# One core, a graph network in one launch: the ranks of the second edge sort made in the edge pass, where they were made beside the attention and the mixer pass

## What is computed

```python
xn = _layernorm(x)
x = x + gnn0(xn, [src, dst], edge_weight) + mix0(xn)     # messages = xn[dst] * w, summed by src
x = x + ffn0(_layernorm(x))                              # 32 experts, one per token
xn = _layernorm(x)
x = x + gnn1(xn, src, dst, deg ** -0.5) + mix1(xn)       # xn[src] summed by dst
x = x + ffn1(x)                                          # 6 experts, two per token
```

## Time and profile before

| | |
|---|---|
| median of 3 runs | 6301.56 us (6300.48 to 6309.79) |
| profiled execution | 6297.91 us, span 6295.7 us |
| PE busy | 5271.7 us, 84% |
| DVE busy | 3384.1 us, 54% |
| POOL busy | 3878.9 us, 62% |
| ACT busy | 1311.4 us, 21% |

### The profile page before, as it was taken

One profiled execution on the slowest core, in us unless ns is written; L12 is line 12 of the kernel. 1 busy time (PEld: TensorE's weight loads), 2 busy tenths in 40 slices (PEclk: granted clock), 3 DMA queues, 4 the chain that ended last, 5 costly groups with the idle time before them and its releaser, 6 DMA issues.

```text
span 6295.7 us, 87281 instructions
## 1 busy us (share of the span) xinstructions
PE 5271.7 (84%) x24977; PEld 4430.6 (70%) x24977; DVE 3384.1 (54%) x9879; ACT 1311.4 (21%) x2962; POOL 3878.9 (62%) x4349
## 2 busy tenths in 40 slices
PE   0165766499999999989999899999999999987894
PEld 0154655267777777777888787778887788866782
DVE  9866666445555555455446544555455554547223
ACT  0011111011111111133224322331112311111340
POOL 5767777765655555688888883316763167636006
PEclk9976888699999999999999999999999999998995
DMA  1022122233333333611001101223332144453324
GB/s 43 24 79 81 55 63 58 83 104 98 100 99 98 101 98 98 69 46 42 17 16 39 39 17 27 82 65 100 104 100 80 62 114 114 109 95 96 97 89 133
DMA packets 319773, 477.58 MB, mean 76 GB/s; under 512 B 99008, under 2 KB 240054, under 8 KB 319470
## 3 DMA queue, kind: packets, MB, share of 16 engines
q0 software_dynamic: 153136, 262.81, 17.0%
q1 hardware_dynamic: 166334, 211.17, 10.9%
HBM read 371.27 MB, written 102.33 MB: 75 GB/s over the span
## 4 chain that ended last, share of the span: by engine, by line
PE 68%; DMA 10%; POOL 8%; DVE 8%; issue 4%; ACT 1%; DVEq 0%; SPq 0%; ACTq 0%; POOLq 0%
PE bank L2384 18%; PE bank L2395 14%; POOL scratch_sorted L1013 7%; DMA scratch_sorted<-sb_FREE 6%; PE bank L2430 6%; PE bank L2445 6%; PE bank L2612 5%; PE bank L2594 5%; PE bank L2881 3%; PE bank L2737 3%; PE bank L2375 2%; DMA sb_rows<-scratch_xn,sb_row_of 2%; PE bank L2923 1%; DVE sb_STATE L1498 1%; DMA sb_HT<-scratch_ys,sb_srec 1%
## 5 line engine op out<-in xcount | busy, mean ns | idle before, releaser
L1020 POOL DMA_INDIRECT sb_rows<-scratch_xn,sb_row_of x1760 | 1718.4, 976 | 1430.9 <-PE bank L2430 605.5
L1013 POOL DMA_INDIRECT scratch_sorted<-sb_FREE x1564 | 1608.2, 1028 | 486.8 <-issue 330.6
L2395 PE MATMUL bank<-sb_work_FT,sb_W 128*128 128x250 f32 x4400 | 1008.9, 381 | 20.4 <-ACT sb_work_FT L1100 16.0
L1100 ACT ACTIVATE sb_HT<-bank,sb_cols 128x250 f32<-128x250 f32 x1333 | 553.7, 467 | 1979.1 <-PE bank L2594 1060.9
L2395 PEld LDWEIGHTS bank<-sb_work_FT,sb_W 128*128 128x128 f32 x4400 | 846.5, 193 | 135.7 <-ACT sb_work_FT L1100 23.5
L2384 PE MATMUL bank<-sb_W,sb_HT 128*125 128x256 f32 x4000 | 893.4, 380 | 0.7 <-ACT sb_HT L1100 0.7
L2384 PEld LDWEIGHTS bank<-sb_W,sb_HT 128*125 128x125 f32 x4000 | 752.5, 188 | 115.0 <-ACT sb_HT L1100 1.1
L2445 PE MATMUL bank<-sb_rows,sb_work_TM 128*125 128x257 f32 x1760 | 471.4, 392 | 72.7 <-DMA sb_rows<-scratch_xn,sb_row_of 72.2
L1822 DVE TENSOR_TENSOR sb_STATE<-sb_STATE,bank 125x257 f32 x440 | 185.5, 422 | 623.0 <-PE bank L2445 594.1
L1767 DVE TENSOR_TENSOR sb_FREE<-sb_FREE,bank 125x257 f32 x440 | 185.8, 422 | 620.1 <-PE bank L2430 584.8
L2430 PE MATMUL bank<-sb_rows,sb_work_TM 128*125 128x257 f32 x1760 | 440.1, 389 | 34.4 <-DMA sb_rows<-scratch_xn,sb_row_of 25.2
(11 more groups left out here) (392 smaller groups left out, 7008.5 us busy)
## 6 DMA issues: line engine op xcount, KB each, us to landing
sb_rows<-scratch_xn,sb_row_of POOLq DMA_INDIRECT x1760, 2.8
scratch_sorted<-sb_FREE POOLq DMA_INDIRECT x1564, 2.4
scratch_qT<-sb_work_QF SPq DMA_DIRECT2D x100, 250.0 KB
sb_work_QF<-scratch_qT SPq DMA_DIRECT2D x100, 250.0 KB
sb_work_XC<-in_x SPq DMA_DIRECT2D x50, 250.0 KB
sb_work_ZT<-scratch_xn SPq DMA_DIRECT2D x50, 250.0 KB
sb_W<-in_L_mix_W SPq DMA_DIRECT2D x9, 1024.0 KB
sb_work_XC<-scratch_zs SPq DMA_DIRECT2D x28, 256.0 KB, 2.6
```

The source lines that it names most:

```text
L1013: nc.gpsimd.indirect_dma_start(out=sorted_d[e], out_offset=bass.IndirectOffsetOnAxis(ap=pos[e][0:n, c:c + 1], axis=0), in_=rec[e][0:n, 2 * ...
L1020: nc.gpsimd.indirect_dma_start(out=rows[:, t % RING, 0:D], out_offset=None, in_=table, in_offset=bass.IndirectOffsetOnAxis(ap=row_of[:, t: ...
L1100: return nc.scalar.activation(dst, source, func, **k)
L2395: ins = nc.tensor.matmul(dst[:, b, :], w[:, k0 + k, 128 * (b0 + b):128 * (b0 + b) + 128], source[:, k, :], start=(n == 0), stop=(n == 2 * ...
```

## The change

The ranks of the second sort are no longer made in A0 and B0. In A0 the 25 rounds keep only the is-equal, which now also writes its sum (the counts); the running count, the copy and the predicated copy go. From these counts the groups and bases come as before, and a copy of the bases is kept. `sort_start` and `sort_place_second` go from B0; behind B0 the blocks of the edges are copied to a place that the clearing of `STATE` does not reach.

In C0 each of the 25 chain steps gets six DVE operations of 782 columns, for two blocks: two is-equals, two running counts that start from the block's base, and two predicated copies. Each stands alone between two units. After `body_c0(23)`, the last body with a chain, six operations make the slots, and the second scatter on POOL waits for them.

```diff
-            def sort_rank(e, k):
-
-                before = SORT_BASE[e] + PREPARED
-                dve.wait_ge(sort_step, k * 4 + before)
-                nc.vector.scalar_tensor_tensor(is_b, half, iota_b[:, bass.ds(k, 1)], step_of, ALU.is_equal, ALU.mult)\
-                    .then_inc(sort_step, 1)
-                nc.vector.tensor_tensor_scan(scan, is_b, tmp, 0.0, ALU.add, ALU.add).then_inc(sort_step, 1)
-                nc.vector.tensor_copy(packed[:, bass.ds(k, 1)], scan[:, EC - 1:EC]).then_inc(sort_step, 1)
-                nc.vector.copy_predicated(rank, is_b.bitcast(I32), scan).then_inc(sort_step, 1)
...
+            def sort_second_count(k):
+
+                dve.wait_ge(sort_step, k + SECOND_READY)
+                nc.vector.scalar_tensor_tensor(is_b, half, iota_b[:, bass.ds(k, 1)], step_of, ALU.is_equal, ALU.mult,
+                                               accum_out=packed[:, bass.ds(k, 1)]).then_inc(sort_step, 1)
...
+            def sort_second_keep():
+
+                dve.wait_ge(sort_step, SECOND_KEPT - 2)
+                nc.vector.tensor_copy(blk_kept, blk).then_inc(sort_step, 1)
+                nc.vector.memset(at_kept, 0.0).then_inc(sort_step, 1)
+
+            def sort_second_place(c, n):
+
+                j, stage = n % 2, n // 2
+                b = 2 * c + j
+                before = SECOND_KEPT + 6 * c + n
+                dve.wait_ge(sort_step, before - (0 if n == 5 else 1 if c or n else 0))
+                if stage == 0:
+                    ins = nc.vector.tensor_scalar(is_kept[j], blk_kept, iota_b[:, b:b + 1], None, ALU.is_equal)
+                elif stage == 1:
+                    ins = nc.vector.tensor_tensor_scan(counts_kept[j], is_kept[j], is_kept[j], base_kept[:, b:b + 1],
+                                                       ALU.add, ALU.max)
+                else:
+                    ins = nc.vector.copy_predicated(at_kept, is_kept[j].bitcast(I32), counts_kept[j])
+                ins.then_inc(sort_step, 1)
+
+            def sort_second_slots():
+
+                dve.wait_ge(sort_step, SECOND_PLACED - 6)
+                step, at, slot = steps(SECOND_PLACED - 6), at_kept, is_kept[0]
+                step(nc.vector.tensor_scalar(at, at, -1.0, None, ALU.add))
+                step(nc.vector.tensor_scalar(slot, at, 63.5, 1.0 / 128, ALU.subtract, ALU.mult))
+                step(nc.vector.tensor_scalar(slot, slot, ROUND, ROUND, ALU.add, ALU.subtract))
+                step(nc.vector.scalar_tensor_tensor(at, slot, -128.0, at, ALU.mult, ALU.add))
+                step(nc.vector.scalar_tensor_tensor(at, at, float(NS), slot, ALU.mult, ALU.add))
+                step(nc.vector.tensor_copy(pos[1], at))
...
-            def sort_start(k):
-
-                before = SORT_BASE[1] + BASED
-                for j, buffer in enumerate((is_b, is_b2)):
-                    nc.vector.tensor_scalar(buffer, blk, iota_b[:, bass.ds(2 * k + j, 1)],
-                                            base[:, bass.ds(2 * k + j, 1)], ALU.is_equal, ALU.mult)\
-                for j, buffer in enumerate((is_b, is_b2)):
-                    nc.vector.tensor_tensor(start, start, buffer, ALU.add)\
...
             def body_a0(i, slots, after):
-                rank_beside(i, 0)
+                count_beside(i, 0)
...
-                rank_beside(i, 1)
+                count_beside(i, 1)
...
-                start_beside(i, 0)
...
-                start_beside(i, 1)
...
             pairs_next(dve, begin_b0, body_b0)
-            sort_place_second()
             sort_blocks(1)
-            dve.wait_ge(sort_step, SORT_END)
+            sort_second_keep()
+            dve.wait_ge(sort_step, SECOND_KEPT)
...
                 units(1)
+                place(0)
...
                 units(2)
+                place(1)
                 units(3)
+                place(2)
                 if chain:
                     wait(dve, c0_pe.done("g", c))
...
                 units(4)
+                place(3)
                 if chain:
                     scale_c0("", c)
...
                 units(5)
+                place(4)
                 units(6)
+                place(5)
                 if chain:
                     wait(dve, c0_pe.done("logit", c))
...
             for j in range(-2, NC + 1):
                 body_c0(j)
+                if j == NC - 2:
+                    sort_second_slots()
```

More of the change, by code:

```diff
@@ L1404, in sort_prepare_second @@
                 f0, f1 = fields_of(1)
-                step = steps(SORT_BASE[1])
+                step = steps(SECOND_BEGUN)
                 blocks_of_keys(step, dst_i)
@@ L1452, in slots_placed @@
                 step(nc.vector.scalar_tensor_tensor(at, at, float(NS), slot, ALU.mult, ALU.add))
-                step(nc.vector.tensor_copy(pos[e][:, columns], at))
+                step(nc.vector.tensor_copy(pos[0][:, columns], at))
             def sort_first_strips():
@@ L1473, in sort_first_strips @@
                     step(nc.vector.tensor_reduce(start[:, columns], strip_own.rearrange("p b c -> p c b"), AX.X, ALU.add))
-                    slots_placed(step, 0, columns)
+                    slots_placed(step, columns)
             def sort_first_rest():
@@ L1505, in sort_first_rest @@
                 dve.wait_ge(sort_step, FIRST_PLACED - 5)
-                slots_placed(steps(FIRST_PLACED - 5), 0, columns)
-            def sort_rank(e, k):
-                before = SORT_BASE[e] + PREPARED
-                dve.wait_ge(sort_step, k * 4 + before)
-                nc.vector.scalar_tensor_tensor(is_b, half, iota_b[:, bass.ds(k, 1)], step_of, ALU.is_equal, ALU.mult)\
-                    .then_inc(sort_step, 1)
-                dve.wait_ge(sort_step, k * 4 + (before + 1))
-                nc.vector.tensor_tensor_scan(scan, is_b, tmp, 0.0, ALU.add, ALU.add).then_inc(sort_step, 1)
-                dve.wait_ge(sort_step, k * 4 + (before + 2))
-                nc.vector.tensor_copy(packed[:, bass.ds(k, 1)], scan[:, EC - 1:EC]).then_inc(sort_step, 1)
-                hold(dve)
-                nc.vector.copy_predicated(rank, is_b.bitcast(I32), scan).then_inc(sort_step, 1)
[L1521 to L1532, removed]
+                slots_placed(steps(FIRST_PLACED - 5), columns)
             def sort_groups(e):
@@ L1550, in sort_groups @@
                 step(nc.vector.scalar_tensor_tensor(base, base, float(GR), BEFORE, ALU.mult, ALU.add))
-            is_b2 = lane
-            def sort_start(k):
-                before = SORT_BASE[1] + BASED
-                for j, buffer in enumerate((is_b, is_b2)):
-                    dve.wait_ge(sort_step, k * 4 + (before + j - 1))
-                    nc.vector.tensor_scalar(buffer, blk, iota_b[:, bass.ds(2 * k + j, 1)],
-                                            base[:, bass.ds(2 * k + j, 1)], ALU.is_equal, ALU.mult)\
-                        .then_inc(sort_step, 1)
-                for j, buffer in enumerate((is_b, is_b2)):
-                    dve.wait_ge(sort_step, k * 4 + (before + 2 * j + 1))
-                    nc.vector.tensor_tensor(start, start, buffer, ALU.add)\
[L1565 to L1572, removed]
+                if e == 1:
+                    step(nc.vector.tensor_copy(base_kept[:], base))
             def sort_blocks(e):
-                step = steps(PLACED_AT[e])
+                step = steps(BLOCKS_AT[e])
                 step(nc.vector.tensor_copy(baseT[:], BASET))
@@ L1678, in _ @@
             make_context("A0")
-            sort_decode(1)
+            sort_second_counted()
             sort_groups(1)
@@ L1870, in blocks_of, with place @@
                             for t in range(2)]
+                def place(n):
+                    if chain:
+                        sort_second_place(c, n)
                 if chain:
```

49 lines of the change are left out of this document (26 added, 23 removed).

## The result

The changed kernel takes 6421.19 us (median of 4 runs, 6412.63 to 6421.96), the kernel before 6302.27 in the same runs: a ratio of 1.0181, 95% interval 1.0169 to 1.0194. It is slower as forecast, by 119 us in the medians. The profiled execution's span is 6418.9 us, 123.2 more than before, where the sum of the prediction had 90.

What follows compares the result with a forecast made beforehand. POOL's scatters were taken to bound the stretch before C0, and TensorE to bound C0. From 6297.9 us, 25 gained and 115 lost gave 6388 us, 1.4% slower; range 6335 to 6430.

Steps and rivals of the forecast that it cites:

- C0's start, 25 us gained: A0 and B0: POOL's scatters go faster without the removed DVE operations; 25 us gained, ends 10 and 49.
- z 2.3 us later: Each C0 step: the two scans delay z by 2.3 us, so PE's wait grows from 1.28 to 3.6 us.
- The copy, 0.8 us: Each C0 step: the second predicated copy, ahead of the logits, gives PE a new wait of 0.8 us.
- The clock, 1.7 us: Each C0 step: the longer wait for z drops PE to 1.2 GHz for a stretch, costing 1.7 us.
- the 3.18: PE's 3.18 us wait for z in C0's first step, with slower matmuls behind it; evidence for the clock drop.
- The upper end, 3.4: Upper bound of the clock drop's cost in a C0 step: 3.4 us, twice a stretch such as seen.
- The steps: C0: 4.8 us lost a step, counted for 24 of 25 steps, 115 us lost.
- The second scatter, nothing: POOL's second scatter starts 77 us later against C0's end; 86.9 us of idle time hides it, cost nothing.
- The clock did not stay: Rival in C0: the waits come but the clock stays, 75 us lost, 6348 us; chance 0.17.
- The freed POOL: Rival in A0 and B0: scatters reach the clean pace, 145 us gained, 6268 us; chance 0.09.
- The third: Rival: second scatter late (30 us lost) or clock drops twice as long (41 more), 6418 to 6429; chance 0.1.
- DVE finds cover for the running counts: Rival in C0: idle time of 3 us before an add hides the scans, 6293 us, no change; chance 0.04.

Runs made afterwards that it cites:

- e2_copy: e1_idle with the second predicated copy put back ahead of the logits, as in the changed kernel; 6296.00 us in one run.
- e4_scan1: e1_idle with the first running count put back ahead of x1 and the second behind units 5; 6327.09 us in one run.
- e1_fly8: e1_idle with eight scatters in flight in place of four; 6209.57 us in one run, 6213.09 us when timed in rounds (ratio 0.9867).
- e1_idle: The changed kernel with its six operations a step moved to places where DVE waits for PE; 6282.34 us, ratio 0.9974 to the kernel before.
- before_fly8: The kernel before with eight scatters in flight in place of four, nothing else; 6281.98 us, ratio 0.9977.

## Why the prediction was right, and which term was not

- **The number.** The 6421.19 us lie in the stated range of 6335 to 6430, but above my own forecast of 6365 to 6410 (chance 0.6). The mechanism was right, and one term was too small and one path was read wrong.
- **C0's start, 25 us gained.** 23.3. That DVE's saving would not arrive was right. The way was only half right: scatters got shorter (0.99 us for 1.08 in A0), but the pace in A0 did not move, where I had said about 1.4. The gaps took the difference, and the gain came as earlier quiet. The scans are worth some 9 of it, L1564 up to 18 and L1559 up to 7, where the sum had 17, 8 and nothing; each was measured by itself, and they do not add up to 23. That the sum came so near is in part luck: two of its terms were off by a factor of two, one up and one down.
- **z 2.3 us later.** 2.57, with a running count of 1.84 us in place of 1.79. The two steps of that sum were tested apart: the first count alone adds 0.7 us to the wait (I said 0.6), the second 1.8 (I said 1.72).
- **The copy, 0.8 us.** 0.72 in the list of waits, 0.8 a step by e2_copy.
- **The clock, 1.7 us.** This is the term that was mis-sized: "I take 1.7, since the new wait is nearest to the 3.18". A wait of 3.85 us costs 6.2 - 2.57 - 0.72 = 2.9 us. The 1.7 came from another drop, late in C0, behind waits of 0.78 and 1.01 us, and e4_scan1 shows that it fits a wait of 2 us. The upper end, 3.4, was nearer. The first step of C0, which has the 3.18, could have told. Before the change PE is still at half speed 6.4 us after that wait (the row below, 1.90 us is usual), and the lower level lasts some 10 us there (a mean clock of 0.65 from 1291.0 to 1305.6 us). PE also waited for gathers in that step, so it is not the same case; but the drop that I named as the nearest was not the one whose price I took.

```profile
1301.20 3.77 PE L2445 MATMUL bank<-sb_rows,sb_work_TM 128*125 128x257 f32 x8
```

- **The steps.** A full step lost 6.2 us where 4.8 were said, 1.2 of the difference by the clock. I counted 24 such steps; the last two of them lost nothing (50.9 us for 54.8, 41.5 for 41.5), which hid part of the miss. In all C0 lost 133.8 us where 115 were said: 19 of the 33 us by which the profiled span went beyond the sum. The memset is 6 more, C0's start 2, and the 6.6 named above are the rest.
- **The second scatter, nothing.** It started 77 us later against the last mask, as said. But I took POOL's idle time ahead of the gathers for its margin and moved only its end, and not what POOL does behind it: the memset went with it, into DVE's chain, and cost 6.1 us.
- **The rivals.** The clock did not stay. The freed POOL paid only 23 of the ceiling of 145 us; e1_fly8 starts C0 98 us earlier, by another change. The third, 6418 to 6429 with a chance of 0.1, is the one into which the time falls, and its second half came true: the lower level lasts 6.8 us in each step, twice as long as in the drop late in C0. Its first half did not come that way, since the 782 scatters took 1196.0 us in their new place and 1196.2 before; the second pass was delayed by the memset. That DVE finds cover for the running counts was wrong for the places of this change, and right for those of e1_idle.

What stays open: the 6.4 us from L1796 in the second pass to the end, which no single instruction carries. That stretch is 2381.9 us in the one profile of the kernel before, 2388.4 in the changed kernel, and 2383.7 to 2389.5 in the other runs; before_fly8, which differs from the kernel before only in the scatters, has 2383.7, so part of it may not be the change's. It is also open why the wait of 2.0 us in e4_scan1 lowers the clock in most steps and not in all.

## What to carry to other kernels

An engine that is busy half the time still has places that cost in full: read what waits behind each place of its order, and put new work ahead of an instruction that is idle because another engine is late. A saving on an engine that then waits is not lost but stored; ask what it waits for, since the next change (here one number) may set it free. And when a step moves, move in your mind all that its queue issues behind it.

## What the runs showed of the hardware

- A POOL memset in SBUF held a tensor_scalar of DVE to the end of the memset, 7.50 us for 0.17, in 11 of 11 runs in which they met. Ten back-to-back pieces held the first of four to the end of the last piece, so that the four took 10.35 us for 1.38.
- A tensor_tensor of two SBUF inputs and a running count lengthen the indirect DMAs on POOL beside them, from 0.96 to 1.58 and 2.36 us; two beside tensor_scalar took 1.17 and 1.32.
- With eight indirect DMAs in flight the gaps between them were 0.30 us; with four they were 0.54 in A0.
- PE, busy all the rest of the step, took a wait of 1.3 us in each step without a drop of the granted clock, of 2.0 us with a drop in most steps, of 3.2 and 3.85 with one in each step of C0's middle.
